# Attention over a masked graph: q and k parts reach their stacks through DRAM in six transfers, and k's last step moves four rows forward

## The reference

```python
h = relu(layernorm(x))                       # x: 8 x 1024 x 256, float32
q = (h @ Wq + bq).reshape(b, n, 8, 32)       # k and v likewise
scores = einsum('bqhd,bkhd->bhqk', q, k) / sqrt(32)
scores = scores + (1.0 - adj)[None, None] * -1e9     # adj: 1024 x 1024 of 0 and 1
attn = softmax(scores, axis=-1)
out = einsum('bhqk,bkhd->bqhd', attn, v).reshape(b, n, 256)
return x + out @ Wo + bo
```

## Time and profile before

| | |
|---|---|
| median of 3 runs | 1121.21 us (1118.05 to 1121.3) |
| the profiled execution | 1122.66 us, span of the trace 1120.3 us |
| TensorE matmuls busy | 1099.7 us (98% of the span) |
| TensorE weight loads busy | 890.5 us (79%) |
| ScalarE busy | 996.7 us (89%) |
| VectorE busy | 960.2 us (86%) |
| GpSimd busy | 313.0 us (28%) |
| SP's queue of transfers | 95.95 MB, 31.5% of the 16 DMA engines' span |

### The profile page before, as it was taken

How to read it: one execution, slowest core, us unless ns; L and a number is a source line. 1 busy time by engine, 2 the same in 40 slices (tenths; PEclk the granted TensorE clock), 3 DMA queues, 4 the chain that set the end, 5 groups by cost and what they waited for, 6 DMA issues and landing times.

```text
span 1120.3 us, 28439 instructions
## 1 busy us (share of the span) xinstructions
PE 1099.7 (98%) x10736; PEld 890.5 (79%) x10736; DVE 960.2 (86%) x1800; ACT 996.7 (89%) x1833; POOL 313.0 (28%) x505
## 2 busy tenths in 40 slices
PE   8889999999999999999999999999999999999998
PEld 6677877887878888887887877888877888878776
DVE  4778889988889888998889988898889989888886
ACT  2779999999999999999999999999999999999985
POOL 5364122142123222142112422124122142122122
PEclk9889999999999999999999999999999999999999
DMA  6842352423524244342434335243352423424211
GB/s 185 254 112 62 79 136 69 111 67 95 144 67 106 61 122 118 73 108 68 118 96 103 85 77 141 68 111 81 82 139 75 106 71 95 104 67 105 55 30 49
DMA packets 88474, 109.08 MB, mean 97 GB/s; under 512 B 24772, under 2 KB 50628, under 8 KB 88340
## 3 DMA queue, kind: packets, MB, share of 16 engines
q1 hardware_dynamic: 77188, 95.95, 31.5%
q0 software_dynamic: 10960, 11.07, 5.0%
q10 hardware_dynamic: 192, 0.26, 0.1%
HBM read 30.54 MB, written 9.44 MB: 36 GB/s over the span
## 4 chain that ended last, share of the span: by engine, by line
issue 51%; DMA 29%; POOL 15%; SPq 2%; DVE 1%; PE 1%; ACT 0%; POOLq 0%; ACTq 0%; DVEq 0%
DMA inv_rows<-inv_turned 15%; DMA inv_t<-inv_rows 14%; POOL inv_t L469 9%; POOL xn L434 3%; SPq L308 2%; POOL ln_t L419 1%; POOL mask L476 1%; DMA xn<-in_x 0%; PE ps_turn L805 0%; POOL res L439 0%; POOL ln_neg_mean L416 0%; DMA q_stack<-q_lo 0%; POOL ln_var L417 0%; POOL ln_t L423 0%; POOL ln_t L421 0%
## 5 line engine op out<-in xcount | busy, mean ns | idle before, releaser
L590 DVE CUSTOM_DVE_ANT_0 rows<-ps_scores,mask 128x1024 f32<-128x1024 f32 x512 | 615.6, 1217 | 37.0 <-PE ps_scores L765 31.6
L501 ACT ACTIVATE rows<-rows,row_min 128x1024 f32<-128x1024 f32 x512 | 589.7, 1159 | 4.6 <-DVE row_min L590 4.6
L798 PE MATMUL ps_turn<-ident_r,rows_raw 128*128 128x128 f32 x4096 | 466.5, 258 | 10.0 <-ACT turned_a L506 6.5
L798 PEld LDWEIGHTS ps_turn<-ident_r,rows_raw 128*128 128x128 f32 x4096 | 401.6, 141 | 85.5 <-ACT rows L501 25.7
L506 ACT ACTIVATE turned_a<-ps_turn 128x512 f32<-128x512 f32 x512 | 307.7, 601 | 89.5 <-PE ps_turn L798 89.4
L765 PE MATMUL ps_scores<-k_stack,q_stack 128*128 128x512 f32 x1016 | 330.2, 425 | 0.9 <-DVE row_min L590 0.9
L597 DVE COPY turned_b<-ps_turn 128x512 f32<-128x512 f32 x314 | 216.3, 689 | 85.8 <-PE ps_turn L798 80.7
L460 POOL DMA_DIRECT2D inv_rows<-inv_turned x64 | 46.4, 725 | 622.9 <-DVE inv_turned L631 617.5
L469 POOL DMA_DIRECT2D inv_t<-inv_rows x252 | 133.3, 536 | 144.0 <-DMA inv_rows<-inv_turned 139.6
L765 PEld LDWEIGHTS ps_scores<-k_stack,q_stack 128*128 128x128 f32 x1016 | 160.1, 189 | 16.8 <-DVE row_min L590 6.3
L849 PE MATMUL ps_heads<-turned_a,v 128*32 128x256 f32 x2016 | 121.8, 382 | 0.0
(11 more groups left out here) (96 smaller groups left out, 602.4 us busy)
## 6 DMA issues: line engine op xcount, KB each, us to landing
q_stack<-q_hi SPq DMA_DIRECT2D x248, 64.0 KB, 2.0
q_stack<-q_lo SPq DMA_DIRECT2D x248, 64.0 KB, 2.1
k_stack<-k_hi SPq DMA_DIRECT2D x242, 64.0 KB, 2.0
k_stack<-k_lo SPq DMA_DIRECT2D x242, 64.0 KB, 2.0
res<-in_x SPq DMA_DIRECT2D x32, 256.0 KB, 2.7
inv_t<-inv_rows POOLq DMA_DIRECT2D x252, 32.0 KB, 2.3
out<-res SPq DMA_DIRECT2D x31, 256.0 KB, 2.8
xn<-in_x SPq DMA_DIRECT2D x30, 256.0 KB, 3.1
```

Of the source, the lines that this page charges most:

```text
L501: nc.scalar.activation(rows[:, k, :], rows[:, k, :], ACT.Exp, bias=row_min[:, k:k + 1], scale=-1.0, accum_out=row_sum[:, u % 2, j:j + 1]). ...
L590: nc.vector.tensor_tensor_reduce(out=rows[:, k, :], in0=ps_scores[n % 2][:], in1=mask[:, qt, :], scale=1.0, scalar=START_MIN, op0=ALU.add, ...
L798: tr = nc.tensor.transpose(ps_turn[half][:, k, :].bitcast(F32R), rows_raw[:, n % RING, kt * P:(kt + 1) * P], ident_r[:])
```

## The change

Six transfers take the place of 16 in each side step of q or k. SP writes the high tile and the low tile whole to a scratch tensor in DRAM (`parts_out`, 256 KB each), waits until both have landed, and reads them back in four transfers, one for each 32 partitions of the stack, each for all four heads at once (256 KB each). ScalarE's next high part of q (or k) now waits only for the writes to DRAM. TensorE waits once per phase, in slot 28 at the first row, for all of q_stack and k_stack. In both kinds of phases, the step qk 3 (k of the second 512 tokens) takes the place that v 0 or o 0 had (slots 17 to 19), and that step takes qk 3's (slots 21 and 22). The stacking of the start is unchanged but for the names of semaphores.

```diff
@@ STEPS
-     ("v", 0, (17, 18, 19, 19)), ("qk", 3, (21, 21, 22, 22)), ("v", 1, (25, 26, 27, 27)), ("o", 3, (28, 29, 29, 30))),
+     ("qk", 3, (17, 18, 19, 19)), ("v", 0, (21, 21, 22, 22)), ("v", 1, (25, 26, 27, 27)), ("o", 3, (28, 29, 29, 30))),
...
-     ("o", 0, (17, 18, 19, 19)), ("qk", 3, (21, 21, 22, 22)), ("o", 1, (25, 26, 27, 27)), ("v", 1, (29, 29, 30, 30))),
+     ("qk", 3, (17, 18, 19, 19)), ("o", 0, (21, 21, 22, 22)), ("o", 1, (25, 26, 27, 27)), ("v", 1, (29, 29, 30, 30))),
...
+        parts_out = nc.dram_tensor("parts_out", (QK_STEPS, 2, P, BANK), F32, kind="Internal").ap()
...
-        stacked = {n: [[sem(f"{n}_stacked{g}_{h}") for h in range(PARTS)] for g in range(PHASES)] for n in "qk"}
+        bounced = {n: sem(f"{n}_bounced") for n in "qk"}
+        stacked = {n: [sem(f"{n}_stacked{g}") for g in range(PHASES)] for n in "qk"}
+        half_stacked = [sem(f"half_stacked{h}") for h in range(PARTS)]
@@ SP
+            def bounce_step(b, g, s):
+                n, ng = "qk"[s % 2], 1 - g
+                cols = slice(s // 2 * BANK, (s // 2 + 1) * BANK)
+                stack = {"q": q_stack, "k": k_stack}[n][ng]
+                sp.dma_start(parts_out[s, 0], hi[s % 2][:].bitcast(F32)).then_inc(bounced[n], 16)
+                sp.dma_start(parts_out[s, 1], lo[s % 2][:].bitcast(F32)).then_inc(bounced[n], 16)
+                sp.wait_ge(bounced[n], bounce_count(b, g, s) + 32)
+                for r, part in enumerate(parts_of(n, 0, 0, 1, 1)):
+                    sp.dma_start(stack[r * HEAD_DIM:(r + 1) * HEAD_DIM, :, cols].bitcast(F32),
+                                 parts_out[s, part].rearrange("(h d) n -> d h n", d=HEAD_DIM)
+                                 ).then_inc(stacked[n][ng], 16)
+                    if g == 1 and s == 2 and b + 2 < BATCH:
+                        sp.wait_ge(ht_turned, (b + 2) * HT_STEPS)
+                        load_x(b + 2, r)
...
                             sp.wait_ge(lo_done, qk_step(nb, ng, s) + 1)
-                            for h in range(PARTS):
-                                stack_step(sp, ng, s, stacked["qk"[s % 2]][ng], range(h, h + 1))
-                                if g == 1 and s == 2 and b + 2 < BATCH:
-                                    sp.wait_ge(ht_turned, (b + 2) * HT_STEPS)
-                                    load_x(b + 2, h)
+                            bounce_step(b, g, s)
@@ ACT, next_high_part
-                for h in range(PARTS):
-                    if s < 2:
-                        if stack_count(n, g, h, b + 1):
-                            act.wait_ge(stacked[n][g][h], stack_count(n, g, h, b + 1))
-                    else:
-                        act.wait_ge(stacked[n][ng][h], stack_count(n, ng, h, nb, 1))
+                if bounce_count(b, g, s):
+                    act.wait_ge(bounced[n], bounce_count(b, g, s))
+                elif s == 0:
+                    for h in range(PARTS):
+                        act.wait_ge(half_stacked[h], STEP_DMAS * 16)
@@ PE, scores
-                elif i < PARTS:
-                    pe.wait_ge(stacked["q"][g][h], stack_count("q", g, h, fills))
-                    pe.wait_ge(stacked["k"][g][h], stack_count("k", g, h, fills))
+                elif i == 0 and n:
+                    pe.wait_ge(stacked["q"][g], stack_count(g, fills))
+                    pe.wait_ge(stacked["k"][g], stack_count(g, fills))
```

More of the change, by code:

```diff
@@ L290, in slots, with stack_count, bounce_count @@
                         slot(b, g, i, b == 0 and g == 0, b == BATCH - 1)
[L292 to L298, removed]
+        def stack_count(g, fills):
+            return (fills - (1 if g == 0 else 0)) * CHUNKS * PARTS * 16
+        def bounce_count(b, g, s):
+            return (b * PHASES + g) * CHUNKS * 32 + s // 2 * 32
         def parts_of(n, q_hi, k_hi, q_lo, k_lo):
@@ L369, in _ @@
             sp.wait_ge(lo_done, START_QK.index(2) + 1)
-            stack_step(sp, 0, 2, stacked["q"][0])
+            stack_step(sp, 0, 2, half_stacked)
             load_mask(3, MASKS_LATE, TILES)
@@ L756, in scores @@
                 elif n < ROWS and i % (ROWS // CHUNKS) < PARTS:
-                    pe.wait_ge(stacked["q"][g][h], stack_count("q", g, h, fills))
-                elif i < PARTS:
-                    pe.wait_ge(stacked["q"][g][h], stack_count("q", g, h, fills))
-                    pe.wait_ge(stacked["k"][g][h], stack_count("k", g, h, fills))
+                    pe.wait_ge(half_stacked[h], STEP_DMAS * 16)
+                elif i == 0 and n:
+                    pe.wait_ge(stacked["q"][g], stack_count(g, fills))
+                    pe.wait_ge(stacked["k"][g], stack_count(g, fills))
                 if n >= 2:
```

## The result

The changed kernel takes 1126.98 us (median of 4 runs, 1126.2 to 1129.12), the kernel before 1119.99 us beside it (4 runs, 1118.05 to 1121.3). The ratio is 1.0059, 95% interval 1.0042 to 1.0076: 0.59% slower. The forecast was 1127.2 us and 6.0 us more.

A forecast was written before the change was run, and what follows sets the result against it. TensorE was taken to set the pace. The profiled 1122.66 us plus 6.0 for the move, with the transfers and start taken as 0, gave 1128.7, carried to a median of 1127.2 us; range 1119.5 to 1132.

The forecast's parts named there:

- The cost on the path: Slots 20 to 22: qk 3's high part ahead of copy a delays TensorE's turns, 0.40 us a phase, 6.0 us total.
- The lower bound of 0.13: Least cost of the move per phase, in us, read from what slots 4 to 6 lose.
- rival (a): Slots 20 to 21: the wait is hidden, only 2.0 us lost, 1123.2 us, no measurable change; chance 0.25.
- The low part and the side bank: Slots 20 to 21: VectorE's low part is done before the side step; cost nothing, if later at most 0.1 us a phase.
- The other parity: Slot 20 in phases of the other parity: same order, ScalarE as late, the same 0.40 us a phase.
- The transfers: SP's two writes and four reads: step in place after 8.1 us, some 15 us of room before slot 28, cost 0.
- The chain of the inverses: POOL's inv_t lands by 631.6, the product needing it runs at 634.87: 3.3 us of cover beside k's last reads.
- Rival (b): Slot 26: the burst delays inv_t beyond its cover, VectorE stalls; 1 us in 15 phases gives 1142 us; chance 0.11.
- The start: First bounce at 49.5 us, DMA engines saturated: new transfers ease or worsen it, -1.8 to +1.8 us, taken as 0.
- rival (c): Saturated start: inv_t earlier, clock doesn't drop, 3 to 4 us less; 1117.5 us with no move cost; chance 0.09.
- (d): Slot 28: k's last step isn't there, 1 us a phase and more, above 1136 us; chance 0.02.

The follow-up runs named there:

- Run 1: The kernel before with the new order of steps alone, its 16 transfers and waits per head kept: 1127.04 us, ratio 1.0046.
- run 2: The changed kernel with the old order of steps, so the six transfers alone: 1143.85 us, ratio 1.0183.
- run 5: The changed kernel with the high part of k's last step computed for 256 of 512 columns only: 1128.47 us, ratio 1.0059.
- run 10: The changed kernel with one more 128 x 256 activation into a scratch tile ahead of k's last high part: 1132.48 us, ratio 1.009.
- run 6: The changed kernel with the high part of k's last step behind copy a in slot 20: 1130.05 us, ratio 1.0069.
- run 4: The changed kernel with the loads of x moved out of step qk 2, behind the store of o 0: 1124.22 us, ratio 1.0025.
- run 8: The kernel before, unchanged, run again for a second profile of its start: one time, 1118.58 us.
- run 7: The kernel before, with SP waiting for the first two res loads to land before the first step's transfers: 1119.88 us, ratio 0.9987.
- run 3: The changed kernel with one copy per phase given from ScalarE in slot 18 to VectorE, one taken back in slot 23: 1134.79 us, ratio 1.0103.
- run 9: The kernel with later x loads, with k's last step in slots 17, 19, 20, 20 and v 0 or o 0 in 22, 22, 23, 23: 1154.91 us.

## Why the prediction was right, and where it wasn't

**The cost on the path: right, and shown.** I worked out 0.40 us a phase from the delay of 0.58, the 0.71 from copy to load, and 0.14 that come back. Measured: 0.57, 0.72, 0.13, and 0.42 in the mean; 15 x 0.42 = 6.3 us against 6.0. My delay of the turn in slot 21 was 0.42. It is 0.46: the turn loads 1.27 us after the scores before it, where it was 0.81; the gap of 0.51 holds the usual 0.05 between two loads. The second gap, in front of the turn of slot 22, is 0.21 us in phases of the second kind, but isn't marked in those of the first. Run 1 has it with the move alone, run 2 without the move hasn't, and runs 5 and 10 change it by changing nothing but ScalarE's time in slot 20. The lower bound of 0.13 (slots 4 to 6) didn't hold: rival (a) is out.

**The low part and the side bank: half right.** At the measured place it costs nothing. But I wrote "at most some 0.1 us a phase" if it were later. In run 6 it comes some 0.3 us later and the side step waits 0.29 us for it, so there is next to no cover.

**The other parity: right.** Third units of both kinds of phases are 16.96 to 17.01 us.

**The transfers: mis-sized, harmless for slot 28.** I had 8.1 us for a step. The four reads land in the median 3.1 to 3.3, 3.9, 4.7 and 5.2 to 5.4 us after their issue, in this order, instead of 2.0 to 2.8: the first is near the 2.8 us of a single load, and each one behind it takes some 0.5 to 0.8 us more. k's last writes take 2.0 and 2.3 us where nothing is queued in front, and 3.6 and 4.3 behind x; issues from and to DRAM take 0.43 us, not 0.6. So k's last step is in place 9.2 to 10.4 us after its first write in the phases without x, near the 8 to 10 that I gave, but 11.4 to 13.4 in those with x (12.3 in phase 1 of batch 1, from 283.18 to 295.4). The 15 us of room took that. Without the move it costs 1.9 us a phase (run 2).

**The chain of the inverses: wrong.** This is the step that failed, in two places. The first is the cover. I had 3.3 us, from the median landing of 2.3 us of the whole page. In the very phase that I read, the last inv_t landed after 3.4 us, at 632.7, so there were 2.2 us, and in the worst phases of that trace 1.1. The second is what comes on top. Even without x the last inv_t is in place 1.7 us later in the mean in run 4 than in run 1, whose transfers are the old ones; that still fits under the cover, with 0.0 to 1.8 us left. In the second kind of phases step qk 2 carries 1 MB of x between its reads. In phase 1 of batch 1 the last of q's reads lands at 285.9, while k's writes have been on their way since 283.18; so k's reads start beside inv_t instead of ahead of it. In phase 1 of batch 4, changed kernel, inv_t then lands as follows (the view by tile):

```profile
DMA to landing us min/median/max: 3.8/5.1/6.0
```

Rival (b), to which I gave 0.11, did happen, but in part: in six phases and not 15, with 0 to 1.6 us each, 3.7 us in the profiled execution. The queue behind a moved step holds also what was there before; I had named x as waiting, and not as making others wait. The rule that I cited from the Trainium skill, DMA: Bandwidth & Descriptors, Queues, rings and completion order, has the completion count wait for every earlier write of the same DMA engine, whichever queue that came from. It fits: inv_t is POOL's and the reads are SP's, and in run 4 they still delay it. But sharing the DMA engines is enough to explain it as well; no run separates these.

**The start: wrong, as a zero and as a bound.** I had -1.8 to +1.8 us. With six transfers phase 0's first half is shorter by 2.8 us (means of the profiles listed under run 8; the ranges nearly touch), and the sign that I gave for rival (c), a first phase shorter by over 2 us, did show. I had named the clock in (c), but given it no price of its own. In the traces the granted clock is at 1.2 GHz for 13.7, 10.2 and 3.4 us of that half with 16 transfers (kernel before twice, run 1) and for 3.4 or 6.8 us with six. As an estimate, from the two profiles of the kernel before (3.4 us more of it, 1.79 us more in the second unit), such time costs half its length. With that taken off, the three profiles with 16 transfers are at 35.1 to 38.2 us and the eight with six at 33.6 to 36.2, which overlap. So part of the difference goes with the clock. What makes it fall isn't shown: before the fall at 59.96 in the kernel before, matmuls were busy for only 0.62 of 2 us (58 to 60), but in run 1 they were busy for 0.51 of 2 us (62 to 64) and it didn't fall.

```profile
58.00:60.00 2.00, 0.62 (x5) 0.40 (x4) 1.90 (x8) 0.60 (x1) 1.93 (x2) 0.99 0.86 193
```

```profile
62.00:64.00 2.00, 0.51 (x4) 0.39 (x4) 1.76 (x4) 0.34 (x2) 2.00 (x1) 1.00 0.42 103
```

That SP stays silent while it waits for the writes, and leaves the full DMA engines to inv_t and x, is what I argue for the rest; run 7, which imitates only that, shortens the second unit but its total isn't clear of noise. How much of rival (c) is in the timed difference stays open.

So the total is right partly by luck, because two errors nearly cancel: +6.3 for the move, about +4 for the inverses, about -3 for the start, against 6.0 forecast and 7.0 between the medians.

**Rivals (c) and (d)** as outcomes didn't come: the start's gain is smaller than the move's cost, and nothing waits in slot 28 in the changed kernel.

## What to carry to other kernels

Where one engine is full and its queue is fed row by row, a step that is moved carries its helpers' time with it: look for the instruction of the full engine that comes due next in the new slot, and count the delay of exactly that one. A place that costs nothing on one engine may cost on two others (runs 3, 6 and 9), so the new slot has to be read on each of them. And take the cover of a hidden chain from every kind of phase, above all from the one with the most transfers queued, and from the last landing there, not from the median of the page.

## What the runs showed that I had not expected

- Transfers queued together wait for each other: of four reads of 256 KB issued within 1.7 us the first lands 3.1 to 3.3 us after its issue and the last 5.2 to 5.4, while single loads of the same size (res) take 2.8.
- Up to the second unit, executions of one kernel differ by more than all later phases together: 30.82 and 32.37 us to the first copy, 19.53 and 21.32 us for that unit, against 0.1 us over the rest. The granted clock goes with it: of 23 timed executions of the kernel before, the nine with a mean clock of 0.990 to 0.992 took 1121.8 to 1124.5 us, the five with 0.997 or 0.998 took 1117.5 to 1120.9.
- A gap ahead of TensorE's weight loads costs a little less than its length, by the same 0.09 us in three runs: 0.29, 0.51 and 0.87 us of gap cost 0.20, 0.42 and 0.78 us of the unit. 0.05 of that is the usual distance between two loads.
